# A three-layer recurrence in one wavefront: the input groups of layers 1 and 2 made in one step each, with lags of 17 and 34 steps instead of 18 and 36

## What is computed

```
x = x + L0(x)      # gated recurrence
x = x + L1(x)      # h = tanh(x_t @ Wx + b + h @ Wh)
x = x + L2(x)      # the same form, its own weights
x = x + L3(x)      # causal attention, 16 heads, one image key ahead
```

```
fused = sigmoid(concat([x_t, h]) @ w_W + w_b)          # reset, update
memory = x_t @ wx_W + wx_b + reset * (h @ wh_W + wh_b)
h = update * h + (1 - update) * tanh(memory)
```

## Time and profile before

| | |
|---|---|
| median of 3 runs | 3801.61 us (3795.7 to 3803.07) |
| the profiled execution | 3799.08 us |
| its span, first to last instruction | 3797.4 us |
| instructions | 171102 |
| PE matmul busy | 3741.3 us (99%) |
| PE weight load busy | 2490.5 us (66%) |
| DVE busy | 2355.5 us (62%) |
| ACT busy | 1101.2 us (29%) |
| POOL busy | 39.0 us (1%) |
| granted TensorE clock, mean | 0.997 of full speed |

### The profile page before, as it was taken

How to read it: one execution, slowest core, us unless ns; L and a number is a source line. 1 busy time by engine, 2 the same in 40 slices (tenths; PEclk the granted TensorE clock), 3 DMA queues, 4 the chain that set the end, 5 groups by cost and what they waited for, 6 DMA issues and landing times. The chain is left out here.

```text
span 3797.4 us, 171102 instructions
## 1 busy us (share of the span) xinstructions
PE 3741.3 (99%) x77841; PEld 2490.5 (66%) x77841; DVE 2355.5 (62%) x8897; ACT 1101.2 (29%) x3973; POOL 39.0 (1%) x192
## 2 busy tenths in 40 slices
PE   8999999999999999999999999999998999999998
PEld 6776776666777766667667776676654555555555
DVE  4666666666666666666666666666644776766765
ACT  3211111111111111111111111111113666665565
POOL 0000000000000000000000000000000000000000
PEclk9999999999999999999999999999999999999999
DMA  6000000000000000000000000000010000000000
GB/s 204 9 4 4 3 4 3 3 3 4 3 3 4 3 3 3 4 3 3 4 3 4 3 4 3 4 4 3 37 38 4 10 13 12 12 15 12 13 10 21
DMA packets 35141, 47.47 MB, mean 13 GB/s; under 512 B 5808, under 2 KB 22240, under 8 KB 34416
## 3 DMA queue, kind: packets, MB, share of 16 engines
q1 hardware_dynamic: 31776, 30.23, 2.6%
q10 hardware_dynamic: 2640, 6.29, 0.5%
HBM read 28.12 MB, written 8.39 MB: 10 GB/s over the span
## 5 line engine op out<-in xcount | busy, mean ns | idle before, releaser
L254 PE MATMUL bank<-wh,h 128*16 128x256 f32 (+1 forms) x16960 | 982.5, 372 | 7.6 <-ACT h L357 6.9
L232 PE MATMUL bank<-wh,states 128*8 128x256 f32 x16352 | 976.1, 379 | 4.3 <-DVE states L484 4.3
L254 PEld LDWEIGHTS bank<-wh,h 128*16 128x16 f32 (+1 forms) x16960 | 486.7, 96 | 321.8 <-ACT h L357 25.1
L232 PEld LDWEIGHTS bank<-wh,states 128*8 128x8 f32 x16352 | 444.8, 90 | 341.1 <-DVE states L484 16.6
L456 DVE STREAM_TRANSPOSE tp<-bank 128x256 f32<-128x256 f32 x512 | 230.5, 450 | 602.5 <-PE bank L232 600.9
L238 PE MATMUL bank<-wh,states 128*8 128x128 f32 x16352 | 540.0, 273 | 0.0
L238 PEld LDWEIGHTS bank<-wh,states 128*8 128x8 f32 x16352 | 447.1, 90 | 108.1
L362 ACT ACTIVATE gates_sb<-pre_sb 128x32 f32<-128x32 f32 x512 | 117.4, 229 | 1204.0 <-DVE pre_sb L458 1204.0
L273 PE MATMUL bank<-probs_extra,w_qkv 128*32 128x128 f32 x11904 | 393.1, 273 | 0.0
L273 PEld LDWEIGHTS bank<-probs_extra,w_qkv 128*32 128x32 f32 x11904 | 339.9, 110 | 64.2
L357 ACT ACTIVATE h<-sum 128x64 f32<-128x64 f32 (+1 forms) x530 | 135.0, 255 | 775.0 <-DVE sum L408 775.0
(11 more groups left out here) (138 smaller groups left out, 3451.7 us busy)
## 6 DMA issues: line engine op xcount, KB each, us to landing
rows<-in_x_dram SPq DMA_DIRECT2D x32, 256.0 KB, 3.0
out_dram<-X SPq DMA_DIRECT2D x32, 256.0 KB, 2.6
w_qkv<-in_L_cond_c_attn_w_dram SPq DMA_DIRECT2D x1, 3072.0 KB, 11.2
w_qkv<-in_L_cond_w_W_dram ACTq DMA_DIRECT2D x2, 1024.0 KB, 7.5
wh<-in_L_cond_w_W_dram ACTq DMA_DIRECT2D x1, 2048.0 KB, 16.8
wx<-in_L_cond_Wx_dram SPq DMA_DIRECT2D x2, 1024.0 KB, 7.1
wh<-in_L_cond_Wh_dram SPq DMA_DIRECT2D x2, 1024.0 KB, 10.1
wx<-in_mask_Bx1x1xS_ff_dram SPq DMA_DIRECT2D x8, 256.0 KB, 3.3
```

The lines of the kernel that those rows point to most:

```text
L232: mm = pe.matmul(mem.ps0[32 * j:32 * j + B, 0:2 * P], state[:, k, :], columns_of(mem.wh0[:, k, 0:3:2, :], j), start=(k == 0), stop=(k == K ...
L254: mm = pe.matmul(mem.ps12[32 * j:32 * j + B * len(ls), P * l0:P * l1], h12[:, k, (n - 1) % HR, l0:l1, :].rearrange("p l b -> p (l b)"), co ...
```

## The change

Both lags are one and two steps shorter: 17 and 34 instead of 18 and 36, and there are 546 steps instead of 548. The four groups of layer 1 stand in one step, t = 0, and the four of layer 2 in the step behind, t = 1. Before, layer 1 had two in t = 0 and two in t = 1, layer 2 two in t = 2 and two in t = 3. The sums of layers 1 and 2 move from t = 2 and t = 4 to t = 1 and t = 2. DVE's waits for its own keeps move with the lags: they stand at t = 1 and t = 2 where there was one at t = 2. Layer 0's groups, one in each step from t = 4 on, its sum at t = 0, and the code of `fills`, `keep_fills` and `chunk_sum` are as before.

```diff
-LAG12 = [CH + 2, 2 * (CH + 2)]
+LAG12 = [CH + 1, 2 * (CH + 1)]
 STEPS = T + LAG12[1]
...
     m, t = divmod(n, CH)
-    if t < 2 and 0 <= m - 1 < NCH:
-        return [(1, m - 1, 2 * t + g) for g in range(2)]
-    if 2 <= t < 4 and 0 <= m - 2 < NCH:
-        return [(2, m - 2, 2 * (t - 2) + g) for g in range(2)]
+    if t < 2 and 0 <= m - 1 - t < NCH:
+        return [(1 + t, m - 1 - t, g) for g in range(KC)]
     if t >= 4 and m + 1 < NCH:
         return [(0, m + 1, t - 4)]
...
-    layer = {0: 0, 2: 1, 4: 2}.get(t)
+    layer = {0: 0, 1: 1, 2: 2}.get(t)
...
-                if n and n % CH == LAG12[0] % CH and n12[n]:
+                if n and n % CH in (LAG12[0] % CH, LAG12[1] % CH) and nfill[n]:
                     dve.wait_ge(s.fill_kept, nfill[n])
```

## The result

The changed kernel takes 3807.68 us (3801.94 to 3814.23, 18 runs), the kernel before 3798.42 (3792.55 to 3803.07, 18 runs). The ratio is 1.0026, 95% interval 1.002 to 1.0033: slower by 7.6 to 12.5 us. I forecast slower, by about 21. The profiled execution took 3812.86 (span 3811.0).

The account below looks back on a forecast made before the run. PE was taken to bound the kernel, with layer 0's 4.49 us chain holding steps without groups; chunks +23.2, ramp +3.1 and end -5.4 gave +20.9 on 3799.1, so 3820.0, put at 3821; range 3806 to 3836.

Parts of the forecast that it names:

- Groups are filler, the chain is 4.49 and holds the empty steps: Steps without a group: layer 0's recurrence (matmuls, transpose, gates, tanh, state) takes 4.49 us, 0.16 above PE's 4.33.
- VectorE's queue at t = 2: At t = 2, four keeps and layer 2's sum make L456 0.52 late; the step takes 4.98 us, 0.49 above 4.49.
- second rival, the queue that hides it: Steps t = 2 and 3 both take 4.49 because keeps start earlier; +7, 3808 us; chance 7%.
- Keeps overlap at 0.26: In VectorE's queue, a keep of 0.35 us costs 0.26; without overlap, four would cost 1.40.
- ScalarE's copy: At t = 3, the copy of the next input rows (1.12 us) precedes the gates; slack 0.44, no cost.
- The ramp: The two ramp chunks, m = 1 and m = 2, cost +1.0 and +2.0, together +3.1 us.
- The end: Behind layer 0's last step, 34 steps instead of 36 save 5.4 us, with bounds -4 and -7.
- Loads at no cost: SP's loads, tied to group counts at steps 496 and 514 and to states, come at the same place: no cost.
- The clock: Granted clock 9 tenths or more in every slice, so all at the 2.4 GHz level; it should stay there.

Follow-up runs that it names:

- after_loads: The changed kernel with SP's loads of the attention's and the image's weights moved off the four-group steps; 3806.35 us, ratio 1.0023 to the kernel before.

## Why the prediction was right in kind and wrong in size

- *Groups are filler, the chain is 4.49 and holds the empty steps.* Right: 7.82, 7.82, and 4.49 at t = 3. Most of PE's extra work is free there (0.05 of 0.32 shows), and refilling the steps gives the 0.34 a chunk back. In the 28 middle chunks this is 9.5 of the 12.0 to 12.2 us that were lost; the late sum is the other 2.6.
- *VectorE's queue at t = 2*: the step that failed. I put 0.49 on it, 29 x 0.49 = 14 us; it is 0.09, 2.6 us. The mechanism is there, its size is not. Of the some 0.4 too much, 0.26 is the state's distance from L456: I took 2.26 from a step in which the transpose was on time (1065.56 to 1067.82) and carried it to a late one. Part of the 2.26 is DVE waiting for the update matmuls of L238, and a late queue uses this wait up. The trace of before had it, in a row that I did not ask about:

```profile
1060.36 0.32 DVE L463 STREAM_TRANSPOSE tp<-bank 128x128 f32<-128x128 f32 x1 [0.16 <-PE bank L238]
```

- The other 0.16 is the sum: in the parts that the new lag gives (448 and 64 columns) it takes 1.13, not 1.18, and L454 starts 0.08 before its end, where I had 0.03 behind it.
- *The range.* My second rival, the queue that hides it, said 3808, and had 7%. Of my cases it came nearest, for a reason that I had not seen: the keeps are not earlier, but a second wait behind the first takes most of the lateness. Its condition did not hold (t = 2 takes 4.58, not 4.49), and that 3807.68 falls on its 3808 is partly luck: its sum has no stalls beside the loads, and the medians lie nearer together than the kernels at equal clock. The lower end of the term was in the text, and I set the chance by the rows of the queue alone.
- *Keeps overlap at 0.26.* Right, four cover 1.13. The rule of the Trainium skill weighed in the prediction (VectorE: DVE Perf Modes, "The DRAIN you can't avoid") doesn't hold for them. The prediction left out that the same section also says that a next operation which is not held starts earlier; the trace, with a start every 0.26 for 0.35 us each, agrees with that.
- *ScalarE's copy.* Right: it starts 0.97 after S and ends at 2.07, the gates start at 2.73.
- *The ramp*: +3.1 forecast, +3.5 to +3.7 measured; step 16 took 6.7 to 6.9 instead of 6.09, with a gap of issue.
- *The end*: -5.4 forecast (its three parts add up to -5.5), -4.0 to -4.4 measured, -4.7 in after_loads. Step 513 took 7.51 and 7.89 instead of 6.39, which is what is missing. Steps 533 on gave the 4.1.
- *Loads at no cost*: wrong by some 2.6 us, 1.2 to 1.5 in steps 496 to 511 and 1.1 to 1.5 in step 513. Their place in SP's order is the same, but what PE does beside them is not.
- *The clock*: the page has 9 tenths or more in each of 40 slices, and I called all of it the 2.4 GHz level. That holds for the scan. The attention has short stretches at the 1.2 GHz level that a slice hides.

With the queue's term at 0.09 the sum would have been 20.9 - 11.6 = +9.3; the medians differ by 9.3. That is luck. The stretches of the scan and the runs at equal clock give 12 to 13; the corrected sum lacks the stalls beside the loads (2.6), the ramp's excess (0.4 to 0.6) and 0.03 a chunk, and the medians lie nearer together than the runs at equal clock.

## What to carry to other kernels

A step that is held by its matmuls may be under a chain that lies just below. Before moving work out of such a step, find a step of the same kernel without the work and read its length there; where PE's work falls under the chain, the difference becomes waiting, and here a quarter of a group in each emptied step was enough to avoid it. When an instruction gets late, do not carry on the distance to the end of the chain from a step in which it is on time: read every wait between the two, since the largest slack behind it comes off the lateness.

## What the runs showed of the hardware

- Four VectorE instructions of 0.35 us each, from PSUM, cover 1.13: 0.26 apiece. Small ones (24 columns) come every 0.15.
- PE lost 0.42 us to issue in step 496 while a load of 3 MB held the DMA engines at a share of 1.00 (414 GB/s), and 0.91 in step 513, 1.5 us after a load of 2 MB had ended (share 0.00). Waiting for two steps' groups more with the 3 MB load removed the gap in step 496.
- The same eight fp32 matmuls of 512 columns took 6.73 us at a granted clock of 0.50 and 3.67 at 1.00, in two executions of one kernel, both behind 3.21 us of idle PE.
- The attention stage, with no change in it, took between 918.5 and 927.6 us in twelve profiles, where the 28 middle chunks repeated to 0.2 us. Most of the spread of the times is there, and it follows how long the clock was at 0.50.
